# Two buffer pairs instead of one for the four summed blocks of a seven-product pair

## The reference

```python
x1, x2 = x[:, :5120], x[:, 5120:]
h1 = leaky_relu(layer_norm(x1 @ W1.T))      # W1: 256 x 5120; leaky_relu(v) = max(0.05 v, v)
h2 = leaky_relu(layer_norm(x2 @ W1.T))
h1 = leaky_relu(layer_norm(h1 @ W2.T))      # W2: 64 x 256
h2 = leaky_relu(layer_norm(h2 @ W2.T))
h = leaky_relu(layer_norm(concatenate([h1, h2]) @ W3.T))   # W3: 8 x 128
y = h @ W4.T                                # W4: 1 x 8
```

## Time and profile before

| what | value |
|---|---|
| median of 3 runs | 237.23 us (237.14 to 237.43) |
| the profiled execution's own time | 237.35 us |
| its span in the profile | 235.6 us |
| TensorE (PE) busy | 227.2 us, 96% of the span |
| VectorE (DVE) busy | 194.6 us, 83% |
| ScalarE (ACT) busy | 152.9 us, 65% |
| mean granted clock of TensorE | 0.995 of full speed |
| bytes read | 47.8 MB, 203 GB/s over the span |

### The profile page before, as it was taken

The page is one execution under the profiler, slowest core; times in us unless marked ns, Lnnn a source line. Parts: engine busy times, 40 slices in busy tenths (PEclk is TensorE's granted clock), DMA queues, the critical chain, the costliest instruction groups (busy, mean ns, idle before and its releaser), DMA issues.

```text
span 235.6 us, 2891 instructions
## 1 busy us (share of the span) xinstructions
PE 227.2 (96%) x1022; PEld 181.4 (77%) x1022; DVE 194.6 (83%) x246; ACT 152.9 (65%) x242; POOL 7.9 (3%) x16
## 2 busy tenths in 40 slices
PE   7999999999999999999999999999999999999992
PEld 2687777888888777887778887888888888888772
DVE  1679999979889999996669499999989899949424
ACT  5797989689496596973667318546555577515630
POOL 1000000000000000000000310000000000000004
PEclk9999999999999999999999999999999999999998
DMA  5999978877867577657624444688584705050000
GB/s 193 373 416 412 390 268 274 265 225 271 273 224 250 200 237 222 226 173 223 259 88 115 164 170 178 189 273 330 192 267 163 271 14 178 0 178 4 0 0 1
DMA packets 13550, 47.99 MB, mean 204 GB/s; under 512 B 1888, under 2 KB 2272, under 8 KB 11744
## 3 DMA queue, kind: packets, MB, share of 16 engines
q1 hardware_dynamic: 13536, 47.81, 58.5%
HBM read 47.80 MB, written 0.00 MB: 203 GB/s over the span
## 4 chain that ended last, share of the span: by engine, by line
PE 63%; DVE 20%; ACT 7%; issue 3%; DMA 3%; SPq 2%; POOL 1%; POOLq 0%; DVEq 0%; ACTq 0%
PE acc L886 58%; DVE xe_lo L608 5%; DVE xt_lo L608 3%; DMA xe_raw<-x 3%; ACT xe_hi L491 2%; DVE x_sum L661 2%; DVE we_lo L625 2%; PE acc L1008 2%; PE acc L1021 2%; ACT xt_hi L491 2%; DVE xr_lo L608 1%; ACT unused L445 1%; DVE ws_lo L616 1%; DVE x_sum L666 1%; ACT we_hi L451 1%
## 5 line engine op out<-in xcount | busy, mean ns | idle before, releaser
L886 PE MATMUL acc<-xe_lo,we_hi 128*128 128x512 f32 x176 | 68.9, 392 | 0.7 <-DVE xe_lo L608 0.6
L886 PE MATMUL acc<-xe_hi,we_lo 128*128 128x512 f32 x176 | 68.5, 389 | 0.0
L491 ACT CAST xe_hi<-xe_raw 128x1024 fp32r<-128x1024 f32 (+1 forms) x47 | 47.9, 1026 | 29.9 <-PE acc L886 25.0
L608 DVE TENSOR_TENSOR xe_lo<-xe_raw,xe_hi 128x1024 fp32r<-128x1024 f32 (+1 forms) x47 | 55.5, 1199 | 12.7 <-ACT xe_hi L491 12.7
L886 PE MATMUL acc<-xe_hi,we_hi 128*128 128x512 f32 x176 | 48.4, 391 | 0.3 <-DVE stage L710 0.3
L886 PEld LDWEIGHTS acc<-xe_lo,we_hi 128*128 128x128 f32 x176 | 33.0, 188 | 9.0 <-issue 2.3
L886 PEld LDWEIGHTS acc<-xe_hi,we_hi 128*128 128x128 f32 x176 | 32.8, 188 | 7.6 <-issue 1.0
L886 PEld LDWEIGHTS acc<-xe_hi,we_lo 128*128 128x128 f32 x176 | 33.0, 188 | 6.7
L491 ACT CAST xt_hi<-x_sum 128x2048 fp32r<-128x2048 f32 x14 | 26.8, 1911 | 16.0 <-DVE x_sum L671 16.0
L608 DVE TENSOR_TENSOR xt_lo<-x_sum,xt_hi 128x2048 fp32r<-128x2048 f32 x14 | 32.0, 2289 | 1.9 <-ACT xt_hi L491 1.9
L886 PE MATMUL acc<-xt_lo,ws_hi 128*128 128x512 f32 x64 | 25.0, 391 | 0.0
(11 more groups left out here) (98 smaller groups left out, 249.6 us busy)
## 6 DMA issues: line engine op xcount, KB each, us to landing
xe_raw<-x SPq DMA_DIRECT2D x51, 512.0 KB, 4.3
xs_raw<-x SPq DMA_DIRECT2D x14, 1024.0 KB, 5.2
stage<-w SPq DMA_DIRECT2D x21, 256.0 KB, 5.0
xe_raw<-x SPq DMA_DIRECT2D x2, 256.0 KB, 3.4
stage<-w SPq DMA_DIRECT2D x2, 128.0 KB, 2.9
w_raw<-w SPq DMA_DIRECT2D x1, 64.0 KB, 3.9
w_sb<-w SPq DMA_DIRECT2D x1, 8.0 KB, 3.7
w_sb<-w SPq DMA_DIRECT2D x1, 16.0 KB, 3.8
```

What stands on the lines that cost most here:

```text
L491: act.copy(hi_of(u, part), raw_of(u, part)).then_inc(hi_ready[part.buffer], 1)
L608: dve.tensor_tensor(lo_of(u, part), raw_of(u, part), hi_of(u, part).bitcast(F32), ALU.subtract)\
L886: return pe.matmul(acc[:, bank, :], w, x, start=first, stop=True, skip_group_check=True)
```

## The change

The buffer pair T becomes two, T0 and T1, of two blocks (1024 columns) each. The four sums of an S unit are then two parts: T0 has the sums 0 and 1, and T1 the sums 2 and 3. Each has its own cast, its own subtraction and its own three semaphores. The cast of T0 waits for `two_sums_ready`, that of T1 for `sums_ready`. TensorE does the two products of T0 (two hi-by-hi matmuls, then four with a lo) and then those of T1. H, L and D units put their first half in T0 and their second in T1. The size of all buffers together stays the same, and so do the matmuls.

```diff
--- before.py
+++ after.py
@@ -89,16 +89,16 @@
             if kind == "S":
                 pair = seen["S"]
                 seen["S"] += 1
-                wanted = [("R", pair, 0, (0, 1, 2)), ("T", pair, 0, (0, 1, 2, 3))]
+                wanted = [("R", pair, 0, (0, 1, 2)), ("T0", pair, 0, (0, 1)), ("T1", pair, 0, (2, 3))]
             else:
                 pair = seen["E"] + (SEVEN if g == 0 else BOTH)
                 seen["E"] += 2 if kind == "D" else 1
                 if not units:
                     wanted = [("E0", pair, 0, (0,)), ("E0", pair, 0, (1,)), ("E1", pair, 1, (0, 1))]
                 elif kind in "HL":
-                    wanted = [("T", pair, 0, (0, 1)), ("T", pair, 1, (0, 1))]
+                    wanted = [("T0", pair, 0, (0, 1)), ("T1", pair, 1, (0, 1))]
                 elif kind == "D":
-                    wanted = [("E0", pair, 0, (0, 1)), ("T", pair + 1, 0, (0, 1)), ("T", pair + 1, 1, (0, 1)),
+                    wanted = [("E0", pair, 0, (0, 1)), ("T0", pair + 1, 0, (0, 1)), ("T1", pair + 1, 1, (0, 1)),
                               ("E1", pair, 1, (0, 1))]
                 else:
                     wanted = [("E0", pair, 0, (0, 1)), ("E1", pair, 1, (0, 1))]
@@ -166,9 +166,9 @@
         xs_raw = sb("xs_raw", [P, S_RING, 4 * NC])
         xe_raw = sb("xe_raw", [P, E_RING, 2 * NC])
         x_sum = sb("x_sum", [P, 4 * NC])
-        x_hi = {"R": sb("xr_hi", [P, 3 * NC], F32R), "T": sb("xt_hi", [P, 4 * NC], F32R),
+        x_hi = {"R": sb("xr_hi", [P, 3 * NC], F32R), "T0": sb("xt0_hi", [P, 2 * NC], F32R), "T1": sb("xt1_hi", [P, 2 * NC], F32R),
                 "E0": sb("xe0_hi", [P, 2 * NC], F32R), "E1": sb("xe1_hi", [P, 2 * NC], F32R)}
-        x_lo = {"R": sb("xr_lo", [P, 3 * NC], F32R), "T": sb("xt_lo", [P, 4 * NC], F32R),
+        x_lo = {"R": sb("xr_lo", [P, 3 * NC], F32R), "T0": sb("xt0_lo", [P, 2 * NC], F32R), "T1": sb("xt1_lo", [P, 2 * NC], F32R),
                 "E0": sb("xe0_lo", [P, 2 * NC], F32R), "E1": sb("xe1_lo", [P, 2 * NC], F32R)}
 
         stage = sb("stage", [P, 5 * NC])
@@ -291,11 +291,12 @@
         def raw_of(u, part):
             if u.kind != "S":
                 return xe_raw[:, e_slot(part.half)[0], part.blocks[0] * NC:(part.blocks[-1] + 1) * NC]
-            return xs_raw[:, s_slot(u)[0], 0:3 * NC] if part.buffer == "R" else x_sum[:]
+            return xs_raw[:, s_slot(u)[0], 0:3 * NC] if part.buffer == "R" else \
+                x_sum[:, part.blocks[0] * NC:(part.blocks[-1] + 1) * NC]
 
         def columns_of(u, part):
-            first = 2 * part.c if u.kind != "S" and part.buffer == "T" else 0
-            return slice((first + part.blocks[0]) * NC, (first + part.blocks[-1] + 1) * NC)
+            first = 2 if u.kind == "S" and part.buffer == "T1" else 0
+            return slice((part.blocks[0] - first) * NC, (part.blocks[-1] + 1 - first) * NC)
 
         def hi_of(u, part):
             return x_hi[part.buffer][:, columns_of(u, part)]
@@ -484,6 +485,8 @@
                 elif part.buffer == "R":
                     s, landed = s_slot(u)
                     act.wait_ge(xs_landed[s], landed)
+                elif part.buffer == "T0":
+                    act.wait_ge(two_sums_ready, u.nth + 1)
                 else:
                     act.wait_ge(sums_ready, u.nth + 1)
                 if part.before:
@@ -553,8 +556,8 @@
                         hi(es[4], part)
                     for b in range(B):
                         layer2_end(es[0].g, b)
-                    hi(n, n.parts[0])
-                    hi(n, n.parts[1])
+                    for part in n.parts:
+                        hi(n, part)
                 else:
                     if i == 0:
                         hi(es[2], es[2].parts[0])
@@ -568,10 +571,12 @@
                         if j == 1:
                             end_w(n)
                             hi(n, n.parts[1])
+                            hi(n, n.parts[2])
                         hi(u, u.parts[1])
                     if i == 0 or len(es) == 1:
                         end_w(n)
                         hi(n, n.parts[1])
+                        hi(n, n.parts[2])
                 start_w(after[0])
                 hi(after[0], after[0].parts[0])
                 if len(after) > 1:
@@ -653,7 +658,7 @@
                 s, landed = s_slot(u)
                 dve.wait_ge(xs_landed[s], landed)
                 if u.nth:
-                    dve.wait_ge(lo_ready["T"], SEVENS[u.nth - 1].parts[1].nth)
+                    dve.wait_ge(lo_ready["T0"], SEVENS[u.nth - 1].parts[1].nth)
                 if u.g and SEVENS[u.nth - 1].g < u.g:
                     dve.wait_ge(h2_summed, B * u.g)
                 raw = xs_raw[:, s, :].rearrange("p (a b n) -> p a b n", a=2, b=2)
@@ -663,6 +668,8 @@
 
             def third_sum(u):
                 dve.wait_ge(two_sums_ready, u.nth + 1)
+                if u.nth:
+                    dve.wait_ge(lo_ready["T1"], SEVENS[u.nth - 1].parts[2].nth)
                 dve.tensor_tensor(x_sum[:, 2 * NC:3 * NC], x_sum[:, 0:NC], x_block(u, 2), ALU.add)\
                     .then_inc(third_sum_ready, 1)
 
@@ -687,7 +694,7 @@
             def seven_into(g, k):
 
                 if k == 0:
-                    dve.wait_ge(used["T"], last_seven(g).parts[1].nth)
+                    dve.wait_ge(used["T1"], last_seven(g).parts[2].nth)
                     dve.wait_ge(p1_copied, g + 1)
                     if g == 0:
                         dve.wait_ge(w_lo_ready, w_pieces(FIRST[-2]))
@@ -838,6 +845,7 @@
                         lo(n, n.parts[0])
                 w_lo(n)
                 lo(n, n.parts[1])
+                lo(n, n.parts[2])
                 if crosses(es):
                     variance1(B, 0, B, var1_ps(0, 0, B))
                     dve.wait_ge(h3_summed, B)
@@ -906,7 +914,7 @@
                         pe.wait_ge(drained, 5 * (g - 1) + {P2: 2, P4: 3, P3: 4, Q: 5}[bank])
 
             def seven(u):
-                for part, products in zip(u.parts, (RAW_PRODUCTS, SUM_PRODUCTS)):
+                for part, products in zip(u.parts, (RAW_PRODUCTS, SUM_PRODUCTS[:2], SUM_PRODUCTS[2:])):
                     def x_of(buffers, k):
                         return buffers[part.buffer][:, k * NC:(k + 1) * NC]
 
@@ -937,8 +945,7 @@
                 return multiply(u.g, E_BANK[b][m], w_of(w_los, part, m), x_half(u, part, x_hi, b))
 
             def x_half(u, part, buffers, b):
-                first = 2 * part.c if part.buffer == "T" else 0
-                return buffers[part.buffer][:, (first + b) * NC:(first + b + 1) * NC]
+                return buffers[part.buffer][:, b * NC:(b + 1) * NC]
 
             def eight(u):
                 for part in u.parts:
@@ -975,7 +982,8 @@
                             ins = e_lo(u, part, b, m)
                         ins.then_inc(block_done, 1)
                 pe.wait_ge(block_done, 4 * (u.g + 1))
-                pe.sem_inc(used["T"], 2)
+                for part in u.parts:
+                    pe.sem_inc(used[part.buffer], 1)
 
             def last_two(u):
```

## The result

The changed kernel took 238.33 us in the median of 15 runs (237.62 to 239.62), the kernel before 237.44 us beside it (237.04 to 239.11). The ratio is 1.0037, 95% interval 1.0022 to 1.0051. A second set of runs of the same two kernels gave 237.91 and 237.24 us, ratio 1.0026, interval 1.0015 to 1.0038. So the split costs 0.67 to 0.89 us. The forecast was 0.38 us and a median of 237.6. Both medians lie in the stated range, the first of them 0.07 us from its upper end. But both are above the 237.70 at which the prediction lets "slower" begin, and it held "no change" for the likeliest outcome: what was found is a small cost.

What follows compares the result with a forecast made beforehand. TensorE was taken to bound the kernel, at its own pace in the second group. Delays of 0.44 us plus 0.05 for a second raise minus 0.11 gained give 0.38 us, median 237.6, range 236.95 to 238.4 us.

Steps and rivals of the forecast that it cites:

- slower: Whole kernel: a median from 237.70 us on, about 0.2% from no change; chance 0.41.
- no change: Whole kernel: time within about 0.2% (0.47 us) of the kernel before; chance 0.49, the likeliest outcome.
- What bounds the kernel, and where a delay reaches TensorE: TensorE's own pace bounds the second group; added casts and subtractions delay it in the first group only, 0.44 us.
- the five casts and two subtractions: First group's S units, on the path to TensorE: 5 x 0.06 + 2 x 0.07 = 0.44 us.
- What one split costs: ScalarE's casts and VectorE's subtractions of T: successors start 0.06 and 0.07 us later per split.
- Rival 1: Casts and subtractions of T: each new instruction costs its whole fixed part, sum 1.14 us, median 238.4; chance 0.14.
- "I take 0.05" for the second raise of T's counter: End of the first group, TensorE: raising two counters in place of one costs 0.05 us, bounds 0 and 0.05.
- The gain near 145 us: Second group: T0 cast in ScalarE's idle time removes TensorE's wait for xt_lo, 0.11 us gained.
- Rival 3: First group: the delays do not reach TensorE; sum -0.11 to 0.1 us, median 237.2; chance 0.18.
- rival 4: First group, 63.54 to 107.61 us: earlier T0 shrinks VectorE's and TensorE's waits; median 236.5 to 236.8; chance 0.10.
- Rival 2: Third sums, casts and subtractions: queue steps are not free, sum 0.38 + 0.5 us, median 238.1; chance 0.08.

Runs made afterwards that it cites:

- run 6: The changed kernel, with VectorE's subtraction of the second half of unit F moved behind the four drains; ratio 1.0017 to the kernel before.
- runs 6 and 7: Run 7: kernel before, with run 6's subtraction move, and TensorE's wait for its own end and T's counter raise behind F's matmuls; ratio 0.9965, 0.8 us less.

## Why the prediction came out as it did

- *What bounds the kernel, and where a delay reaches TensorE.* Right. The two stretches with the five casts and two subtractions hold 0.53 us, with 0.44 forecast, and fourfold splits scaled as the path says: 1.31 us for 15 casts, 0.40 for 6 subtractions. The fourfold subtraction also cost 0.7 us at the very end of the program, which no path explains. No wait for a T buffer arose, and the pace of the second group stayed.
- *What one split costs.* Right for VectorE. Small for ScalarE: 0.08 in place of 0.06 us, 0.10 us over five. The Trainium skill's rule of a fixed part per instruction ("VectorE: DVE Perf Modes", "The TRN2 errata — SBUF-src ops pay a fixed extra latency per instruction") gives, as an estimate from its figures, 0.19 and 0.16 us per split. The records show 0.19 (2 x 1.050 - 1.911) and 0.15; the starts show 0.08 and 0.07. Rival 1, a path that pays it whole, would have cost 1.14 us and is out by the fourfold splits.
- *"I take 0.05" for the second raise of T's counter.* This step failed in size and in its bounds, 0 and 0.05. It costs 0.14 to 0.15 us in the two profiles of the changed kernel and in that of run 6, and 0.23 in the run with one more raise on the kernel before. The bound came from a queue step of VectorE; nothing in the profile of before showed a raise on TensorE, so the whole 0.30 us that TensorE idles with one would have been the safer upper end.
- *What was not in the sum.* The 0.24 us behind the first matmuls of the second group. The prediction took the 0.30 us before 115.43 for TensorE's wait for its own end, which runs 6 and 7 bear out, and gave no thought to the drain that the row names (`stage L710`). It did not ask what stands ahead of them on VectorE, a subtraction that waits for a load, with some 1.1 us to spare: the second drain ended at 114.63 us, and the second matmul of the second group started at 115.74. The drains came 2.05 us later and TensorE 0.89, which uses up the 1.1 us and a little more. This is the largest part of the miss.
- *The gain near 145 us.* Right: 0.11 forecast, 0.17 found for the stretch, and it comes alone with the split in the second group.
- *Rival 3 (delays covered) and rival 4 (faster)* are out. *Rival 2* had the right sign, by steps of the queue at each cast and in the third sum; the stretches leave it no room, and the extra cost stood elsewhere.
- *The total.* That 0.38 came within 0.3 to 0.5 us of the measured cost is not all merit: a term of 0.24 us was missing, the raise and the casts were taken 0.2 us too small together, and the range held the first 238.33 us because it reached to the price of rival 1, a mechanism that the runs rule out. That part is luck.

What stays open: why the load takes 1.3 us longer to land. The packet of the instruction queue is the best candidate and not shown.

## What to carry to other kernels

Splitting an operation in two here cost the difference of the starts of its successors, 0.07 to 0.08 us, at each place where the chain of waits runs through it: count those places and leave the others whole. Here the split helps in the one group where VectorE has time and hurts in the other. Then look at each point where an engine waits for its own last instruction: a second counter raised there cost 0.15 us or more, and moving the wait and the raise behind the next unit's work, together with a subtraction behind the drains, gained 0.6 to 0.8 us, where the split of the second group gained 0.1 to 0.2. For an engine that is released in time, look at what stands ahead of the releaser and how much it has to spare; a load in that place is a risk, whatever the change is about.

## What the runs showed of the hardware

- 18 raises of a counter on TensorE within a stream of matmuls cost nothing that the times show (ratio 1.0002, 0.9984 to 1.0019). A second raise where the engine has just waited for its own last matmul goes with 0.45 to 0.53 us of idle time in four profiles, against 0.30 in six and 0.38 in one with a single raise.
- Added instructions went with a cost far from where they stand: in the one profile with 42 more subtractions, 0.36 us more of unexplained issue time stand ahead of VectorE's last instruction, and the last transfer takes 1.9 us in place of 1.4. No cause was shown.
- The landing of one 512 KB load followed the start of a 16 KB packet of an instruction queue by 2.0 us in the four profiles in which that packet started 2.9 to 3.5 us behind its issue. Another load of the same size, with the packet 2.7 us behind its issue, landed as usual, 3.3 us after it, in two profiles of two. That the packet delays a load is therefore not shown.
